# Probabilities times values in the first attention layer: the values become the stationary operand, and the result comes back through a transpose

## The reference, cut to what matters

```python
qkv = einsum('bse,oe->bso', layernorm(x), Wqkv_w) + Wqkv_b      # q, k, v: 16 heads of 32
q, k = rotary(q), rotary(k)
scores = einsum('bthd,bshd->bhts', q, k / sqrt(32)) + causal_mask
attn = softmax(scores, axis=-1)
out = einsum('bhts,bshd->bthd', attn, v)                          # the changed product
x = x + out.reshape(B, S, 512)
```

## Time and profile before

| | before |
|---|---|
| median of three runs | 1186.12 us |
| the profiled execution | 1186.13 us |
| its span in the trace | 1184.3 us |
| PE, DVE, ACT, POOL busy | 96%, 72%, 69%, 53% |
| first attention, products L938 | 50.7 to 205.3 us |

### The profile page before, as it was taken

One profiled execution on the slowest core, in us unless ns is written; L12 is line 12 of the kernel. 1 busy time (PEld: TensorE's weight loads), 2 busy tenths in 40 slices (PEclk: granted clock), 3 DMA queues, 4 the chain that ended last, 5 costly groups with the idle time before them and its releaser, 6 DMA issues.

```text
span 1184.3 us, 20333 instructions
## 1 busy us (share of the span) xinstructions
PE 1140.3 (96%) x6330; PEld 766.6 (65%) x6330; DVE 852.0 (72%) x2769; ACT 819.9 (69%) x2348; POOL 622.7 (53%) x753
## 2 busy tenths in 40 slices
PE   4889989799999999999999999999999999999998
PEld 2567756566666676677766676667676667554564
DVE  4669978998778876597886867758777786576242
ACT  4677668788878886678767687667777679565130
POOL 1647975654645554275653755426554462357172
PEclk9889989899999999999999999999999999999999
DMA  8211010212111120232123320114311200000000
GB/s 280 90 61 29 24 35 17 89 55 72 55 36 54 61 82 19 90 97 89 46 76 102 98 78 21 58 67 150 118 35 44 67 14 2 1 1 1 36 2 27
DMA packets 28588, 70.39 MB, mean 59 GB/s; under 512 B 3024, under 2 KB 10320, under 8 KB 28480
## 3 DMA queue, kind: packets, MB, share of 16 engines
q1 hardware_dynamic: 28208, 68.72, 18.1%
q10 hardware_dynamic: 272, 0.36, 0.1%
HBM read 61.73 MB, written 7.34 MB: 58 GB/s over the span
## 4 chain that ended last, share of the span: by engine, by line
PE 77%; DVE 9%; POOL 7%; ACT 4%; issue 2%; DMA 1%; ACTq 0%; SPq 0%; POOLq 0%; DVEq 0%
PE ps L969 20%; PE ps L961 11%; PE ps L1066 8%; PE ps L1037 8%; PE ps L1021 8%; PE ps L995 6%; PE ps L1078 4%; PE ps L1004 4%; PE ps L981 4%; POOL big L1838 2%; DVE big L1441 2%; PE ps L992 2%; POOL big L1836 1%; POOL big L1827 1%; ACT big L1185 1%
## 5 line engine op out<-in xcount | busy, mean ns | idle before, releaser
L969 PE MATMUL ps<-big 128*125 128x512 bf16 x1152 | 264.6, 379 | 0.5 <-ACT big L1300 0.5
L1300 ACT ACTIVATE big<-ps,big 112x128 f32<-112x128 f32 (+1 forms) x512 | 192.9, 461 | 33.6 <-POOL big L1864 31.8
L969 PEld LDWEIGHTS ps<-big 128*125 128x125 bf16 x1152 | 154.1, 136 | 79.4 <-ACT big L1300 0.7
L961 PE MATMUL ps<-big 128*112 128x512 bf16 x768 | 186.6, 387 | 2.7 <-ACT big L1300 1.9
L1862 POOL TENSOR_TENSOR big<-big 112x4 f32<-112x4 f32 (+1 forms) x128 | 44.7, 349 | 234.6 <-ACT big L1132 234.4
L1441 DVE BATCH_NORM_STATS2 big<-ps 112x6 f32<-112x128 f32 (+1 forms) x512 | 113.4, 283 | 57.9 <-PE ps L969 44.1
L961 PEld LDWEIGHTS ps<-big 128*112 128x112 bf16 x768 | 99.4, 132 | 65.3 <-issue 6.2
L1874 POOL TENSOR_TENSOR big<-big 128x448 f32<-128x448 bf16 x64 | 67.4, 1054 | 128.5 <-DVE big L1732 128.5
L1021 PE MATMUL ps<-big 125*128 125x224 f32 (+1 forms) x512 | 119.5, 355 | 7.6 <-DVE big L1691 4.0
L1129 ACT ACTIVATE big<-big 112x4 f32<-112x4 f32 (+3 forms) x151 | 45.7, 303 | 104.8 <-DVE big L1449 100.3
L1021 PEld LDWEIGHTS ps<-big 125*128 125x128 f32 (+1 forms) x512 | 92.0, 189 | 26.4 <-DVE big L1691 4.8
(11 more groups left out here) (124 smaller groups left out, 2349.9 us busy)
## 6 DMA issues: line engine op xcount, KB each, us to landing
big<-in_ctx_t SPq DMA_DIRECT2D x32, 375.0 KB, 3.6
big<-in_w_s SPq DMA_DIRECT2D x16, 512.0 KB, 3.7
big<-in_w_p SPq DMA_DIRECT2D x16, 512.0 KB, 3.9
big<-in_w_x SPq DMA_DIRECT2D x16, 512.0 KB, 3.7
big<-in_w_g SPq DMA_DIRECT2D x16, 512.0 KB, 3.7
big<-in_w_d SPq DMA_DIRECT2D x8, 512.0 KB, 4.4
scr<-big SPq DMA_DIRECT2D x28, 128.0 KB, 1.7
big<-scr SPq DMA_DIRECT2D x7, 512.0 KB, 8.6
```

Of the source, the lines that this page charges most:

```text
L961: t = e.matmul(bk[0:T, :], xq[:, k, :], wt[:, s, k, col:col + 512], start=k == s == 0, stop=k == 3 and s == 1)
L969: t = e.matmul(bk[0:CK, :], ctxT[:, s, k, CK * c:CK * c + CK], wt[:, u, k, col:col + 512], start=k == s == u == 0, stop=k == 3 and s == 1)
L1300: t = e.activation(z[0:rows, 128 * j:128 * j + 128], ps(("p_mm", n))[0:rows, 128 * j:128 * j + 128], ACT.Identity, bias=v["q"][:, j:j + 1] ...
```

## The change

`a_s3` turns the operands round: the values of a head (112 rows, 32 columns) are stationary, and its 112 columns of transposed probabilities move through. The result of head 4h + c lies on the partitions 32h to 32h + 31, in the columns 112c to 112c + 111 of the same bank: features on partitions, tokens in columns. The four heads of a group so go to the four quarters of the array's columns. Two steps are new. `a_ot` (ScalarE) copies a batch's bank of 128 x 448 to SBUF after its last group, and `a_tb` (TensorE) turns it back with four transposes (112 stationary columns, 128 moving ones) into a bank of its own. `a_s4` waits for these, and reads with an index order (c, h, d) in place of (h, d). The copy lies in memory that is idle at the time: for the batches 0 to 5 in columns where the quantized tokens of batches 6 and 7 come later, for 6 and 7 in the buffers of the transposed x.

```diff
-    ... (9, "a_te", 1), ("h", 4, "a_s4"), ("h", 2, "a_s2e"), ...
-    ... ("h", 3, "a_s3"), (20, "l_q", 0), (0, "a_h", None), ...
+    ... (9, 'a_te', 1), ('h', 4, 'a_tb'), ('h', 4, 'a_s4'), ('h', 2, 'a_s2e'), ...
+    ... ('h', 3, 'a_s3'), ('h', 3, 'a_ot'), (20, 'l_q', 0), (0, 'a_h', None), ...
@@ a_s3 (PE)
             for h in range(4):
                 hh = 4 * h + c
-                t = e.matmul(ps(("a_s3", b))[0:T, 32 * hh:32 * hh + 32], p[0:T, h, :],
-                             v[0:T, 32 * hh:32 * hh + 32], start=True, stop=True)
+                t = e.matmul(ps(("a_s3", b))[32 * h:32 * h + 32, T * c:T * c + T], v[0:T, 32 * hh:32 * hh + 32],
+                             p[0:T, h, :], start=True, stop=True)
             t.then_inc(pv_a.sem, 1)
+
+        def a_tb(g):
+            if g % 4 == 3:
+                w.wait_ge(*ot_made[g])
+                bk = fresh(("a_tb", g))
+                for c in range(4):
+                    t = e.transpose(bk[0:T, 128 * c:128 * c + 128], a_ot_sb[g // 4][:, c, :], identf)
+                t.then_inc(o_back.sem, 1)
@@ ACT
+        def a_ot(g):
+            if g % 4 == 3:
+                w.wait_ge(*pv_a[g])
+                if g > 3:
+                    w.wait_ge(*o_back[g - 4])
+                e.activation(a_ot_sb[g // 4], ps(("a_s3", g // 4))[:, 0:448].rearrange("p (c t) -> p c t", c=4),
+                             ACT.Copy).then_inc(ot_made.sem, 1)
@@ a_s4 (DVE)
-            w.wait_ge(*pv_a[g])
+            w.wait_ge(*o_back[g])
...
-            e.tensor_tensor(z[0:T, :].rearrange("p (h d) -> p h d", h=16),
-                            ps(("a_s3", b))[0:T, :].rearrange("p (h d) -> p h d", h=16),
-                            sm[0:T, 0:16].unsqueeze(2).broadcast_to([T, 16, 32]), ALU.mult).then_inc(az_made.sem, 1)
+            e.tensor_tensor(z[0:T, :].rearrange("p (h c d) -> p h c d", h=4, c=4),
+                            ps(("a_tb", g))[0:T, :].rearrange("p (c h d) -> p h c d", c=4, h=4),
+                            sm[0:T, 0:16].rearrange("p (h c) -> p h c", h=4).unsqueeze(3).broadcast_to(
+                                [T, 4, 4, 32]), ALU.mult).then_inc(az_made.sem, 1)
```

More of the change, by code:

```diff
@@ L113, in take @@
         return a
[L116 to L123, removed]
+A_PLAN = [(5, 'a_ev', 0), ('h', 2, 'a_s2'), (8, 'a_tq', 0), ('h', 0, 'a_qk'), (9, 'a_tq', 1), (8, 'a_te', 0), (6, 'a_mm', 3), (5, 'a_rot', 0), (7, 'a_ev', 2), (0, 'a_ln', None), (6, 'a_ev', 1), (7, 'a_rot', 1), (2, 'a_tl', None), (4, 'a_mm', 1), (19, 'l_t', None), (0, 'a_rstd', None), (9, 'a_te', 1), ('h', 4, 'a_tb'), ('h', 4, 'a_s4'), ('h', 2, 'a_s2e'), (5, 'a_mm', 2), (17, 'l_ln', None), (1, 'a_tr', None), (17, 'l_rstd', None), ('h', 0, 'a_s0'), (23, 'l_q', 3), (21, 'l_q', 1), (3, 'a_mm', 0), ('h', 3, 'a_s3'), ('h', 3, 'a_ot'), (20, 'l_q', 0), (0, 'a_h', None), (22, 'l_q', 2), (17, 'l_h', None)]
 def first_layer(tick):
@@ L372, in _program @@
     h1 = f32(aH1, 512)
-    a_xT = [b16(aw.take(448), 896).rearrange("p (s k t) -> p s k t", s=2, k=4) for _ in range(2)]
+    aXT = [aw.take(448) for _ in range(2)]
+    a_xT = [b16(a, 896).rearrange("p (s k t) -> p s k t", s=2, k=4) for a in aXT]
     a_q, a_k, a_v = [f32(aw.take(512), 512)], [f32(aw.take(512), 512)], [f32(aw.take(512), 512) for _ in range(3)]
@@ L384, in _program @@
     xqx = b16(aXQX, 4 * 896).rearrange("p (k t) -> p k t", k=4)
+    a_ot_sb = [f32(aXQV, 4 * 448).rearrange("p (c t) -> p c t", c=4)[:, :, 336:448] if b < 6 else
+               f32(aXT[b % 2], 448).rearrange("p (c t) -> p c t", c=4) for b in range(NB)]
     X_K1, X_V1 = aKV, aKV + 1500
@@ L494, in _program @@
     pv_a = signal("pv_a", "a_s3")
+    o_back = signal("o_back", "a_tb", if_=lambda g: g % 4 == 3)
     zT = signal("zT", "l_t")
@@ L515, in _program @@
     pT_a_act = signal("pT_a_act", "a_s2e", if_=lambda g: g % 2 == 1)
+    ot_made = signal("ot", "a_ot", if_=lambda g: g % 4 == 3)
     zl_made = signal("zl", "l_h")
@@ L655, in place @@
                 bank.take((s, k // 4))
+        elif s == "a_ot":
+            if k % 4 == 3:
+                bank.give(("a_s3", k // 4), ot_made[k])
+        elif s == "a_tb":
+            if k % 4 == 3:
+                bank.take((s, k))
         elif s == "a_s4":
@@ L660, in place @@
                     z_slot.give((s, k), x1_made[k])
-                bank.give(("a_s3", k // 4), az_made[k])
+                bank.give(("a_tb", k), az_made[k])
         elif s == "l_h":
@@ L1086, in d_0 @@
                                  stop=True).then_inc(ssq.sem, 1)
-        mine = dict(a_tr=a_tr, a_mm=a_mm, a_tq=a_tq, a_qk=a_qk, a_s2=a_s2, a_s3=a_s3, l_t=l_t, p_mm=p_mm, p_t=p_t,
+        mine = dict(a_tr=a_tr, a_mm=a_mm, a_tq=a_tq, a_qk=a_qk, a_s2=a_s2, a_s3=a_s3, a_tb=a_tb, l_t=l_t, p_mm=p_mm, p_t=p_t,
                     t_s0=t_s0, t_s2=t_s2, t_s3=t_s3, t_s6=t_s6, b_m=b_m, f_1=f_1, g_0=g_0, d_0=d_0)
@@ L1419, in g_1 @@
             e.activation(ffn_h[j][m][0], hf[hf_slot.of[k]][:, 0:W[j]], ACT.Copy).then_inc(hh_made.sem, 1)
-        mine = dict(prep_a=prep_a, a_rstd=a_rstd, a_h=a_h, a_tr=a_tr, a_te=a_te, a_s0=a_s0, a_s2e=a_s2e, l_rstd=l_rstd,
+        mine = dict(prep_a=prep_a, a_rstd=a_rstd, a_h=a_h, a_tr=a_tr, a_te=a_te, a_s0=a_s0, a_s2e=a_s2e, a_ot=a_ot, l_rstd=l_rstd,
                     l_h=l_h, l_t=l_t, b_0=b_0, b_m=b_m, p_rstd=p_rstd, p_v=p_v, p_z=p_z, p_t=p_t, p_mm=p_mm, t_s0=t_s0,
```

## The result

The changed kernel takes 1190.93 us (median of 20 runs, 1188.66 to 1193.29), the kernel before 1186.21 (20 runs, 1183.7 to 1189.6). The ratio is 1.0033, 95% interval 1.0025 to 1.0042: about 4 us slower, with the bound of what can be told from no change (0.3%) inside the interval. The forecast was 1187.0 us. The profiled execution took 1189.77 us with a span of 1188.0 (before: 1184.3).

The account below looks back on a forecast made before the run. Before 240 us a chain of waits, GpSimd's alone from 104 to 167, bounds what the change can win; TensorE bounds the rest. Copies 0.42 + 0.42, wait 0.2, bursts -0.2 give +0.8 on 1186.13: 1187.0 us, range 1183.0 to 1193.5.

Parts of the forecast that it names:

- The bound and the place: Effects arise before 240 us and pass on one for one; GpSimd alone is the chain from 104 to 167 us.
- a sign that I had named for a missed mechanism: A wait on L952 over 1 us outside batches 0 and 5, or a difference arising after 240 us.
- The products: TensorE's burst of eight records, running in pairs, costs 0.70 us against 0.78: -0.08 us a burst.
- rival 1: All four quarters run side by side on TensorE: burst 0.50 us, -0.28 each; sum +0.2, 1186.4 us; chance 0.20.
- rival 2: No overlap between TensorE's quarters: burst 1.08 us, +0.30 each; +6.4, 1192.6 us; chance 0.14, 0.02 of it far out.
- The slack, and the point from which rival 2 decides: From 93 to 166 us TensorE can grow 1.8 us free; costs start once a burst costs more than now.
- The transposes and the copy on ScalarE: Four transposes back cost TensorE 0.43 us a batch; ScalarE's copy adds 0.42 on the chain for batches 0 and 5 each.
- The wait of `a_s4` in batch 1: VectorE waits for the transposes before L1540, where it works without a gap: 0.2 us counted (0 to 1.2).
- Batch 5: Result reaches VectorE 4 us later; its 4 us idle time covers this, costed at nothing, up to 4 us without cover.
- The bursts on the chain after 173: Two TensorE bursts on the chain after 173 us, each -0.08: -0.2 us (-0.6 to +0.6).
- The sum: Whole kernel: 0.42 + 0.2 + 0.42 - 0.2 = +0.8 us, forecast 1187.0 us.
- Rival 3: TensorE's half-clock stretches: one or two more, 1189.4 to 1191.8 us, chance 0.09; or one goes, 1184.6, chance 0.04.

Follow-up runs that it names:

- experiment 2: Changed kernel without ScalarE's copy and the transposes back, all four heads writing the same 32 partitions: 1186.33 us, ratio 1.0001 to the kernel before.
- experiment 8: Kernel before, SyncE asking for the next weights ahead of writing batch 0's sum: 1185.62 us, ratio 0.9992; best version of the change with this edit: 1186.06, 0.9997.
- experiment 5: Changed kernel, batch 5's copy one tick sooner and transposes first in TensorE's tick: 1188.09 us, ratio 1.0012; with batch 6's early too: 1188.15, 1.0016.
- experiment 7: Changed kernel; in tick 37 VectorE makes the projection's statistics ahead of `a_s4`, GpSimd `p_rstd` ahead of `l_q`: 1189.57 us, ratio 1.0026 to the kernel before.
- experiment 1: Changed kernel with the new products alone, no copy or transposes back, `a_s4` reading the products' bank: 1186.06 us, ratio 0.9996 to the kernel before.
- experiment 3: Changed kernel doing all its work, but `a_s4` waits only for the products and multiplies the values tile in SBUF: 1191.02 us, ratio 1.0044 to the kernel before.
- experiment 4: Changed kernel, `a_s4` reading the products' bank, copy two ticks later, transposes into a bank nobody reads: 1196.4 us, ratio 1.009 to the kernel before.

## Why the prediction was right and where it failed

**The bound and the place.** Right. Nothing arises after 240 us; GpSimd's stretch stayed the chain from 104.83, 0.6 later as foretold, to 166.87, and TensorE's saving in it became waiting. But a sign that I had named for a missed mechanism came: waits on L952 of over 1 us outside batches 0 and 5, of 1.7 us on TensorE in batch 1 and of 1.7 and 2.3 us on VectorE in batches 4 and 6.

**The products.** The size was wrong, and rival 1 had it. A burst takes 0.33 us to the next line's start. The way in costs 0.09: nine matmuls of the projection take 126.84 - 124.76 = 2.08 us ahead of a burst, and 127.07 - 125.08 = 1.99 before, by the next burst of the earlier trace rows:

```profile
127.07 0.88 PE L938 MATMUL ps<-big 112*112 112x32 f32 x8
```

From burst to burst that is 4.67 us against 4.95, so 0.28 less, what rival 1 had for four quarters side by side, where the forecast took 0.08. That the difference fits to the hundredth is luck: rival 1 had 0.50 against 0.78, and it is 0.42 against 0.72. The gap ahead of the new weight loads was there, 0.39 us where 0.34 was foretold. Seventeen bursts and four sets of transposes make -4.8 + 1.7 = -3.1. TensorE's busy time from 93 to 166 fell by 4.5 (71.21 to 66.75), and its waits rose by as much: 2.8 for GpSimd (1.8 to 4.6) and 1.7 for the copy of batch 1; how the 4.5 goes with the 3.1 was not followed further. The reason against rival 1, that the two records of a head share a quarter, did not hold; rival 2, which cited the Trainium skill's "TensorE: Matmul & The Clock Gate", Part 3, did not either: by that rule a load would not overlap matmuls of the same rows, and here eight loads and eight matmuls on the same 112 rows take 0.33 us, less than one load and one matmul of L943 end to end (0.11 and 0.28 us, by their medians).

**The slack, and the point from which rival 2 decides.** Wrong, though not in the sum. I said that TensorE's work could grow by 1.8 us and cost from there on. In experiment 2 a burst with what is around it takes 0.2 us more than before (3.14 and 2.04 us for the two parts of the tick, 5.18 against 4.95), 3.9 us over 17, and the kernel was as fast. The wait of TensorE is not all of its slack: in that execution the time that had been lost at the lower clock was there as well, as it was in experiment 8's.

**The transposes and the copy on ScalarE.** Right: 0.44 us for four at full clock (111.84 to 112.28), and 0.43 and 0.44 for the copy on the chain, for batch 0 (net: its 0.56 us come with 0.13 less between the exponentials) and for batch 5. The sum had not foreseen that the transposes of batch 5 would lie on the chain too, at half clock: 1.12 us.

**The wait of `a_s4` in batch 1.** Forecast 0.2; measured 0. The multiply starts 0.65 us behind the one before (95.86 against 95.21), no more than the chain is late anyway. TensorE was at the transposes at 92.94, not at 94.99, and waited until 94.63 for the copy. That is in part luck: in the kernel before the granted clock was 0.50 from 88 to 92, and here it was 1.00.

**Batch 5.** The step that failed, as the prediction put it: "VectorE has 4 us of idle time before its next input from TensorE, and I cost that delay at nothing." The delay came, from 167.61 to 173.36 us (171.8 foretold; 0.7 of the difference is the half clock in the transposes, 1.12 us against 0.44), and the idle time was there. But the cover was that of one engine, and what stood behind `a_s4` in VectorE's queue had consumers elsewhere: `l_q` on GpSimd, behind which `p_rstd` waited, and the projection's statistics, which `p_rstd` needs. The prediction gave "up to 4 us" for the case that the cover is gone and left it out of the sum and out of the rivals. Experiments 5 and 7 show it: with 2.1 us of the lateness gone, 2.5 to 3.8 us are gained, the copy's 0.4 among them, and 0.6 on the chain with a part of the queueing alone gone. The cover held for most of the 2.6 us of lateness that experiment 5 left (0.3 at the eviction of tick 37), not for 4.7 (2.1).

**The bursts on the chain after 173.** Forecast -0.2. In the change they are not on the chain; where they are, in experiment 1, the two save 0.74 us.

**The sum.** +0.8 was 0.42 + 0.2 + 0.42 - 0.2. Measured, by the two profiles: 0.4 for batch 0, 0.5 from the load that landed later in this execution, 0.4 that builds up in GpSimd's stretch, less 0.3 by which this execution was ahead at 65 us (L1586 there at 65.66, L1608 here at 65.34), which makes the 1.0 at 169 us; 2.1 at batch 5; and 0.5 between 215 and 225, where eight matmuls at half clock now lie on the chain:

```profile
219.76 3.41 PE ps L974 x8
```

Before 215 us the shift is 3.1, after 225 it is 3.6. Rival 3 had named such a stretch; I did not test it by itself. These make 3.6. The medians differ by 4.7: the profiled execution of the change is 1.2 us under its median, and where the slower ones lose that no profile shows. The time is in the range, and that is luck: the likeliest case was not the true one, no rival priced the late result of batch 5, and the upper part of the range was there for rivals 2 and 3. The time falls among rival 3's (1189.4 to 1191.8), but half clock accounts for the 0.5 us after 215 and 0.7 of batch 5's delay, not for most of the loss. The loss is at the bound where "no change" ends.

## What to carry to other kernels

An engine's idle time covers a delay only for that engine. Before a late input is called free, follow every instruction queued behind the waiting one to its consumers on the other engines, and the small operations that stand behind those in their queues. And a saving on an engine that waits for another is not a saving: 32 shorter bursts gave nothing, while one copy in the wrong place of a queue cost 2.5 to 3.8 us.

## What the hardware showed that I had not expected

- Four float32 products whose results lie in four different quarters of the partitions overlap: eight records in 0.33 us, 0.88 us when all use one quarter (and the same addresses), on the same rows.
- A VectorE multiply of 512 columns with both operands in SBUF took 1.69 us beside a GpSimd operation (batch 0 of experiment 3) where it takes 0.69 with one operand in PSUM. In batches 1 to 3 it took 0.69, and the GpSimd operation beside it and the sum with x 1.44 to 1.49 us in place of 1.0.
- A copy and four transposes two ticks later, with the PSUM bank held that long, made the kernel 5.5 us slower than the change (experiment 4), with TensorE waiting 8.3 us at another step; that the bank is the cause is not shown.
- The granted clock between 94 and 166 us did not follow TensorE's busy time: 1.00 with 71.12 us busy (experiment 2) and with 67.37 (experiment 8), 0.97 with 66.36 (experiment 1), and 0.98 in the kernel before, whose work was that of experiment 8.
